# Constant rows of layer 1 from scaled sums on VectorE and products with ones, the first counting round partly in line, and five waits moved

## The chip, the cores and the metric

The kernel runs on one core of one Trainium2 chip. A core has TensorE (matrix products, 128 x 128), VectorE, ScalarE and GpSimd (elementwise work on 128 partitions), SyncE (whose queue starts the DMA transfers here), an SBUF and a PSUM of eight banks of 128 x 512 float32. Each engine has its own instruction stream and meets the others only at semaphores. The metric is the time of the whole launch in device microseconds, the median of three runs.

## The reference

A node matrix x (1024 x 512) passes four residual layers over one graph of 32768 edges, each `x = layernorm(x + layer(x))`:

```
layer 0: adj = 1 where an edge runs either way, + I; scaled by 1/sqrt(degree); adj @ (x @ W0) + b0
layer 1: three graph convolutions in a row without a nonlinearity:
         h = A (x W1) + b1;  h = A (h W2) + b2;  h = A (h W3) + b3
         A = D^-1/2 (counts of edges + I) D^-1/2
layer 2: attention: softmax over the edges of (x Wq + bq)(x Wk + bk)^T / sqrt(512), times (x Wv + bv)
layer 3: relu(A (x W1) + b1), then A (h W2) + b2
```

## The kernel before

**Layer 1 folded.** Because layer 1 has no nonlinearity, its three weights are multiplied into one matrix (units `w12`, `wf`), and the biases become constant rows: `fold1 = b2 W3` and `fold2 = (b1 W2) W3`, each needed on all 128 partitions. Before the change unit `bT` turns the two biases into columns, unit `bw` forms b1 W2 as a column (16 products of one output column each, L653), unit `g` multiplies the two columns with W3 (four products with two weight columns and 512 moving ones, L648), and the 2 x 512 result goes by DMA to DRAM and back, spread over the partitions (L465 to L468).

**The counting round.** The dense count matrix is built from the sorted edges in 64 groups of 512 edges. For each group VectorE and ScalarE make one-hot matrices (`hot_key`, `lo_near` on VectorE; `apart`, `lo_far` on ScalarE), TensorE multiplies them (L697), and VectorE adds the two results at places that are read from a table `base_at` into registers, once for four groups (L1370, L1362). VectorE makes one-hots three groups ahead. Nearly always one round of 64 groups is enough; `rounds` says how many there are.

**Units between the groups.** The dense products that don't need the graph are cut into units of four pieces. A planner deals the pieces out behind the groups of the round (`pieces`): every piece has a weight (`weight_of`), each group brings a credit of `SHARE`, and what is left stands behind the round (`BEHIND`) or between the eight transpositions of the link matrix (`REST`, L742). ScalarE copies every unit's bank out.

**Behind the round.** VectorE turns the counts into `link` (L1422), TensorE transposes it (`turn_links`), VectorE makes `sym`, and layer 0 begins (L770). Layers 1 and 3 stand twice in the program, for small and for large degrees (`big`), each as one `If` and `Else`.

**The softmax of layer 2.** For each of eight tiles VectorE finds the peak and the reciprocal, ScalarE makes exponents and quotients, and TensorE transposes the result (`turn_probs`, L983) between products of the scores (`scores`, seven products M1 to M7 of a fast matrix scheme) and of the mixing (`mix`). All three orders are written out by hand.

## Time and profile before

| | |
|---|---|
| runs, median (lowest to highest) | 546.02 us (545.72 to 546.28) |
| the profiled execution's own time | 545.62 us |
| its span in the profile | 543.8 us |
| TensorE busy | 529.8 us, 97% of the span |
| VectorE busy | 398.3 us, 73% |
| ScalarE busy | 171.7 us, 32% |
| GpSimd busy | 143.1 us, 26% |

The span runs from the first to the last instruction of the execution that the profiler recorded; its own time is 1.8 us longer, for what lies around it. Times in the rows below are microseconds from the span's start. L12 is line 12 of the kernel before. A group of instructions is given with its operation, what it writes and reads, and its count; what stands in brackets behind a row is how long its engine sat idle before it and what ended that ("issue": nothing that the profile shows).

### The profile page before, as it was taken

The numbers are of one execution on the slowest core, as the hardware profiler recorded it, in microseconds if no ns is written. First come the engines' busy times: TensorE is split into PE (matmuls) and PEld (weight loads), VectorE is DVE, ScalarE is ACT, GpSimd is POOL, SyncE is SP. The second block draws the span as 40 slices with busy tenths as digits, with TensorE's granted clock in tenths as the row PEclk, the third lists the DMA queues.
The fourth block names the chain that finished last, engine by engine and source line by source line (L and its number), as shares of the span: only waits on it lengthen the run. The fifth ranks groups of instructions, "written<-read, shape, count | busy, mean of one in ns | idle before, by whom it ended". The sixth has DMA issues, their size and how long they took to land.

```text
span 543.8 us, 7062 instructions
## 1 busy us (share of the span) xinstructions
PE 529.8 (97%) x2317; PEld 373.1 (69%) x2317; DVE 398.3 (73%) x873; ACT 171.7 (32%) x361; POOL 143.1 (26%) x135
## 2 busy tenths in 40 slices
PE   8999999999999999999999999899989999999995
PEld 6555565357788888888674764467678888888643
DVE  6888888789878989355576977897887916690165
ACT  5999896472021022220220000542343100120200
POOL 3000000085228504022224800653400390000021
PEclk9999999999999999999999999999999999999999
DMA  8724000100102012000000000000020300000012
GB/s 290 272 79 153 3 1 0 42 1 0 41 9 107 2 19 79 0 1 0 2 1 0 2 0 0 1 0 1 2 77 0 136 0 1 1 1 0 1 58 99
DMA packets 12763, 20.19 MB, mean 37 GB/s; under 512 B 3243, under 2 KB 3507, under 8 KB 12726
## 3 DMA queue, kind: packets, MB, share of 16 engines
q1 hardware_dynamic: 12726, 19.69, 10.7%
q8 instruction: 24, 0.39, 0.3%
q14 instruction: 13, 0.11, 0.1%
HBM read 17.57 MB, written 2.11 MB: 36 GB/s over the span
## 4 chain that ended last, share of the span: by engine, by line
PE 83%; DVE 8%; ACT 4%; issue 3%; POOL 1%; DVEq 0%; POOLq 0%; ACTq 0%
PE bank L951 13%; PE bank L770 13%; PE bank L955 12%; PE bank L788 11%; PE bank L1011 9%; PE bank L844 4%; PE bank L658 3%; PE bank L697 3%; PE bank L643 3%; PE bank L662 3%; PE bank L666 3%; PE bank L983 1%; DVE wk_rows L1519 1%; PE bank L674 1%; ACT apart L1101 1%
## 5 line engine op out<-in xcount | busy, mean ns | idle before, releaser
L549 POOL TENSOR_TENSOR rstd<-veps,mhalf 128x1 f32<-128x1 f32 x32 | 22.2, 695 | 177.5 <-DVE veps L1450 174.7
L1370 DVE TENSOR_TENSOR count<-bank,count 128x160 f32 x128 | 41.3, 323 | 13.9 <-PE bank L697 7.2
L788 PE MATMUL bank<-adj,y_hi 128*128 128x512 f32 x128 | 51.1, 399 | 0.0
L788 PE MATMUL bank<-adj,y_lo 128*128 128x512 f32 x128 | 50.4, 394 | 0.0
L1457 DVE SCALAR_TENSOR_TENSOR xs<-bank,dinv,xs 128x512 f32<-128x512 f32 x23 | 16.9, 746 | 43.9 <-PE bank L844 30.5
L1101 ACT ACTIVATE apart<-col_lo,edge_key 128x128 bf16<-128x128 int16 x128 | 44.0, 395 | 0.7 <-PE bank L686 0.7
L586 POOL TENSOR_SCALAR mask<-count 128x1024 bf16<-128x1024 uint16 x8 | 23.5, 2931 | 52.3 <-DVE peak L1669 43.5
L1354 DVE TENSOR_TENSOR hot_key<-col_key,key 128x320 bf16<-128x320 int16 x128 | 35.4, 316 | 0.2 <-issue 0.2
L697 PEld LDWEIGHTS bank<-hot_key,lo_near 128*128 128x128 bf16 x128 | 12.0, 100 | 31.8 <-issue 23.4
L658 PE MATMUL bank<-w_sb,x0t 128*128 128x512 f32 x64 | 33.1, 601 | 0.6 <-ACT x0t L1082 0.3
L1108 ACT ACTIVATE lo_far<-apart,ones 128x256 bf16<-128x256 bf16 x64 | 31.9, 500 | 0.0
L534 POOL TENSOR_SCALAR degs<-degs 128x1 f32<-128x1 f32 x8 | 3.5, 441 | 101.1 <-DVE sym L1427 100.7
L788 PEld LDWEIGHTS bank<-adj,y_hi 128*128 128x128 f32 x128 | 24.0, 188 | 6.1 <-DVE wide L1535 0.2
L788 PEld LDWEIGHTS bank<-adj,y_lo 128*128 128x128 f32 x128 | 24.0, 188 | 5.6
L844 PE MATMUL bank<-v_sb,gt 128*128 128x512 f32 (+1 forms) x72 | 27.6, 545 | 0.0
L1535 DVE TENSOR_TENSOR score<-bank,score 128x512 f32<-128x512 f32 x28 | 18.8, 687 | 9.9 <-PE bank L955 9.7
L770 PE MATMUL bank<-ya_hi,sym 128*128 128x512 f32 x64 | 25.4, 397 | 0.0
L770 PE MATMUL bank<-ya_hi,adj 128*128 128x512 f32 x64 | 25.2, 394 | 0.0
L788 PE MATMUL bank<-adj,yb_lo 128*128 128x512 f32 x64 | 25.2, 394 | 0.0
L788 PE MATMUL bank<-adj,yb_hi 128*128 128x512 f32 x64 | 25.2, 394 | 0.0
L770 PE MATMUL bank<-ya_lo,adj 128*128 128x512 f32 x64 | 25.1, 391 | 0.0
L770 PE MATMUL bank<-yb_lo,adj 128*128 128x512 f32 x64 | 25.0, 391 | 0.0
(288 smaller groups left out, 1241.2 us busy)
## 6 DMA issues: line engine op xcount, KB each, us to landing
w_sb<-in_L_gnn_W_dram SPq DMA_DIRECT2D x3, 1024.0 KB, 5.6
xs<-in_x_dram SPq DMA_DIRECT2D x2, 1024.0 KB, 7.1
v_sb<-in_L_gnn_W_dram SPq DMA_DIRECT2D x2, 1024.0 KB, 6.0
out_dram<-xs SPq DMA_DIRECT2D x7, 256.0 KB, 2.0
w_sb<-in_L_gnn_weight_dram SPq DMA_DIRECT2D x4, 256.0 KB, 6.1
wq_sb<-in_L_gnn_Wq_dram SPq DMA_DIRECT2D x1, 1024.0 KB, 10.6
wk_sb<-in_L_gnn_Wk_dram SPq DMA_DIRECT2D x1, 1024.0 KB, 12.8
wq_rows<-in_L_gnn_Wq_dram SPq DMA_DIRECT2D x1, 1024.0 KB, 7.8
```

Of the source, the lines that this page charges most:

```text
L658: mm = pe.matmul(to, x0t[:, k, rows], w0_sb[:, k, :], start=first, stop=last)
L697: return pe.matmul(bank[:, slot, span], lo, hot_key[:, slot, c // PAIR, :, c % PAIR], start=c % PAIR == 0, stop=c % PAIR == PAIR - 1)
L770: mm = pe.matmul(to, m[:, k, j * P:(j + 1) * P], y[part][:, k, :], start=n == 0 and part == 0 and m is mat, stop=n == NB - 1 and part == 1 ...
L788: mm = pe.matmul(to, y[part][:, k, f * P:(f + 1) * P], m[:, k, half], start=n == 0 and part == 0 and m is mat, stop=n == NB - 1 and part = ...
L844: mm = pe.matmul(bank[:, 0 if cols is high_cols else HALF * (s % 2) + b, cols], g(k, j), w[:, k, cols], start=k == 0, stop=k == FB - 1)
L951: mm = pe.matmul(to[:, i * D // 2:(i + 1) * D // 2], b[:, k, rows], a[:, k, :], start=k == 0, stop=k == 1)
L955: mm = pe.matmul(to, a[:, k, n * P:(n + 1) * P], b[:, k, :], start=k == 0, stop=k == 1)
L1011: mm = pe.matmul(mix_bank(m), left[:, k, :], right[:, k, :], start=k == 0, stop=k == HALF - 1)
L1101: ins = nc.scalar.activation(apart[:, n, c - BY_DVE, :], col_lo[:], ACT.Abs, scale=-1.0, bias=edge_key[:, 0, bass.ds(g + c * G, 1)])
L1108: nc.scalar.activation(lo_far[:, slot], apart[:, n], ACT.Relu, scale=-1.0, bias=ones[:, 0:1]).then_inc(act_hot_set, 1)
L1354: V.tensor_tensor(hot_key[:, slot, n], col_key[:], key16[:, bass.ds(g, 1), n * PAIR:(n + 1) * PAIR].to_broadcast([P, KEYS, PAIR]), ALU.is_ ...
L1370: return V.tensor_tensor(count[:, :, bass.ds(at_dst, WIN)], bank[:, slot, n * KEYS:(n + 1) * KEYS].rearrange("p (h d) -> p h d", h=NB), co ...
```

## The change

- `fold1` and `fold2` come without the DMA. VectorE forms sums over the four 128-row blocks of a weight, each block scaled per partition by the bias (`scaled_sum`, `rows_of_biases`): four instructions for b1 W2, four for b2 W3, four for (b1 W2) W3. Units `ra` and `rb` then multiply each sum with a matrix of ones, which adds over the partitions and puts the result on all of them; unit `tc` does the same with one column of ones for b1 W2, which is needed as a column. Units `bT`, `bw` and `g` are gone. The biases are loaded as columns, element by element.
- VectorE's sums stand behind twelve groups of the round (`ROWS_AT`). For that the last 32 of the 64 groups stand in line (16 before), and the first round stands ahead of the loop over rounds; the further rounds are under an `If`, which VectorE passes at the end of the first.
- The number of rounds is found behind the first one-hots, not ahead of them.
- Unit `wf` 0 comes into the round; behind it is unit `rb`. The first three link transpositions wait for their own banks' units only, not for the last.
- The large-degree copies are cut into four smaller `If`/`Else` pairs, with the products `part` standing once between them.
- Softmax: TensorE has the product M1 of tile pair 2 ahead of the first `turn_probs`; ScalarE has `exponents(1)` ahead of `first_part("s", 2)` and `quotients(6)` ahead of `first_mix(2)`; VectorE has `reciprocal(6)` ahead of `add_m57(1)`.

```diff
+ROWS_AT = (33, 35, 37, 39, 41, 43, 45, 47, 53, 55, 57, 59)
...
-        UNITS = x_t[:4] + sum((along[n] for n in range(5)), []) + [("bT", 0, 0)] + along[5]
+        UNITS = x_t[:4] + sum((along[n] for n in range(6)), [])
         UNITS += each("m") + along[6] + along[7]
-        UNITS += [("bw", 0, 0)] + each("w12") + [("g", 0, 0)] + each("wf")
+        UNITS += each("w12")[:1] + [("tc", 0, 0)] + each("w12")[1:] + [("ra", 0, 0)] + each("wf")[:1] + [("rb", 0, 0)] + each("wf")[1:]
...
-                sp.dma_start(brow[n * FB:(n + 1) * FB, :], b.rearrange("(c p) -> c p", p=P)).then_inc(cols_in, 16)
+                sp.dma_start(bcol[:, n, :], b.rearrange("(c p) -> p c", p=P),
+                             allow_slow_non_contiguous=True).then_inc(cols_in, 16)
...
-            sp.wait_ge(unit_out, upto["g"])
-            sp.dma_start(fold_rows[:, :], grow).then_inc(fold_kept, 16)
-            sp.wait_ge(fold_kept, 16)
-            for n, t in enumerate((fold1, fold2)):
-                sp.dma_start(t[:], fold_rows[n, :].partition_broadcast(P)).then_inc(fold_in, 16)
...
+                    pe.wait_ge(row_sums, {"tc": 1, "ra": 2, "rb": 3}[kind])
+                    if kind == "tc":
+                        for c in range(FB):
+                            mm = pe.matmul(to[:, c:c + 1], w2_row[:, c * P:(c + 1) * P], ones[:, 0:1], start=True, stop=True)
+                    else:
+                        mm = pe.matmul(to, ones[:], (fold1 if kind == "ra" else fold2)[:], start=True, stop=True)
...
-                if h == 0:
-                    pe.wait_ge(unit_out, UA + 1)
+                if h < 3:
+                    pe.wait_ge(unit_out, UA - 2 + h)
...
-            def layer1(mats):
...
+            whole_or_apart(lambda more: cols_steps(2, adj, yb, NB, more), rest_l1)
+            for n in range(FOLDED):
+                part(*PARTS[n])
+            whole_or_apart(layer1_rows, rest_l1)
...
+            scores(2, ("M1",))
             turn_probs(0)
-            scores(2, ("M1", "M2", "M6"))
+            scores(2, ("M2", "M6"))
...
             copy_probs(0)
+            exponents(1)
             first_part("s", 2)
-            exponents(1)
...
+            quotients(6)
             first_mix(2)
-            quotients(6)
...
+            def scaled_sum(to, w, by, k):
+
+                if k == 0:
+                    ins = V.tensor_scalar(to, w[:, 0, :], by[:, 0:1], None, ALU.mult)
+                else:
+                    dve.wait_ge(dve_set, chain[0])
+                    ins = V.scalar_tensor_tensor(out=to, in0=w[:, k, :], scalar=by[:, k:k + 1], in1=to,
+                                                 op0=ALU.mult, op1=ALU.add)
...
+            dve.wait_ge(rounds_set, 1)
+            open_round(0)
+            count_rounds()
+            dve.wait_ge(const_set, 3)
+            with dve.Fori(0, G // BODY - 2) as q:
...
+            for n in range(G - 2 * BODY, G):
+                if n % HALF == 0:
+                    places = places_at(n)
+                one_group(n, places[n % HALF], n, n % SLOTS, n + AHEAD if n + AHEAD < G else None)
+                rows_of_biases(n)
+            dve.wait_ge(rounds_set, 2)
+            rounds = dve.value_load(flags[0:1, 0:1], min_val=1, max_val=ROUNDS)
+            with dve.If(rounds > 1):
+                with dve.Fori(1, rounds) as r:
...
             m4("s", 3)
+            reciprocal(6)
             add_m57(1)
-            reciprocal(6)
```

On TensorE, the end of the round before (L697 are the groups' one-hot products, L662 unit `w12`, L648 unit `g`):

```order
L697 MATMUL bank<-hot_key,lo_far 128x160 x2
L662 MATMUL bank<-w1t,w_sb 128x512
L697 MATMUL bank<-hot_key,lo_near 128x160 x2
L697 MATMUL bank<-hot_key,lo_far 128x160 x2
L648 MATMUL bank<-w_sb,gcol 2x512
L697 MATMUL bank<-hot_key,lo_near 128x160 x2
L697 MATMUL bank<-hot_key,lo_far 128x160 x2
L648 MATMUL bank<-w_sb,gcol 2x512
```

and the same place now (L685 the one-hot products, L650 `w12`, L639 `ra`, L654 `wf`):

```order
L685 MATMUL bank<-hot_key,lo_far 128x160 x2
L650 MATMUL bank<-w1t,w_sb 128x512
L685 MATMUL bank<-hot_key,lo_near 128x160 x2
L685 MATMUL bank<-hot_key,lo_far 128x160 x2
L639 MATMUL bank<-fold_131,ones 128x512
L654 MATMUL bank<-w_sb,w12t 128x512
L685 MATMUL bank<-hot_key,lo_near 128x160 x2
L685 MATMUL bank<-hot_key,lo_far 128x160 x2
L654 MATMUL bank<-w_sb,w12t 128x512
```

The four products of `g` are gone from the last groups; one product of `ra` and the first unit of `wf`, which stood behind the round, are there instead.

On VectorE, the end of the round before (count additions of the last group, then `counted` and the link matrix):

```order
L1370 ISA
L1370 TENSOR_TENSOR count<-bank,count 128x8x20
L1388 REGISTER_ALU
L1388 COMPARE_AND_BRANCH
L1410 ISA
L1411 MEMSET rr 128x8
L1422 TENSOR_SCALAR link<-count 128x1024 x8
```

and now, where the rows left out are the 322 of the further rounds, which the branch passes over:

```order
L1358 TENSOR_TENSOR count<-bank,count 128x8x20
L1431 TENSOR_LOAD flags
L1431 ISA x2
L1432 COMPARE_AND_BRANCH
L1433 UNCONDITIONAL_BRANCH
...
L1432 UNCONDITIONAL_BRANCH
L1444 ISA
L1445 MEMSET rr 128x8
L1456 TENSOR_SCALAR link<-count 128x1024 x8
```

A load of the number of rounds and a taken branch over a long stretch of instructions have come between the last addition and the link matrix.

On TensorE, the first transpositions of probabilities now (L974, L983 before), where one product pair L943 (M1) stood behind the first of them before:

```order
L943 MATMUL bank<-xt_sums,tt 128x512 x4
L943 MATMUL bank<-xt,tt 128x512 x2
L974 MATMUL bank<-ident,score 128x128 x8
L943 MATMUL bank<-xt,tt 128x512 x2
L943 MATMUL bank<-xt_sums,tt_sums 128x512 x2
L974 MATMUL bank<-ident,score 128x128 x8
```

M1 has moved ahead of the first transposition; the second stands behind the same products as before.

## Rows read from the trace of the kernel before

**Rows 1.** the page's first part: busy time, share of the span, instructions
```profile
PE 529.8 (97%) x2317; PEld 373.1 (69%) x2317; DVE 398.3 (73%) x873; ACT 171.7 (32%) x361; POOL 143.1 (26%) x135
```

**Rows 2.** the waits of TensorE, whole span: total us, times, longest
```profile
PE bank L983 <- ACT score L1224: 3.2, 3, 1.5
```

**Rows 3.** groups of TensorE's instructions, busy us and mean ns
```profile
L648 PE MATMUL bank<-w_sb,gcol 128*2 128x512 f32 x8 | 3.9, 592 | 0.0
L653 PE MATMUL bank<-bcol,w_sb 128*128 128x1 f32 x32 | 3.8, 240 | 0.0
```

**Rows 4.** the chain: start us, us on it, what
```profile
79.17 0.79 PE bank L653 x8
```

**Rows 5.** timeline of TensorE, end of the round: start us, us, what
```profile
103.39 3.63 PE L666 MATMUL bank<-w_sb,w12t 128*128 128x512 f32 x8
107.70 0.62 PE L742 MATMUL bank<-identb,link 128*128 128x128 bf16 x8 [0.68 <-ACT wfold L1095]
```

**Rows 6.** timeline of VectorE, the round: first count of a group
```profile
60.45 0.33 DVE L1370 TENSOR_TENSOR count<-bank,count 128x160 f32 x1 [1.16 <-issue]
...
65.81 0.32 DVE L1370 TENSOR_TENSOR count<-bank,count 128x160 f32 x1 [0.61 <-issue]
...
71.16 0.33 DVE L1370 TENSOR_TENSOR count<-bank,count 128x160 f32 x1 [0.61 <-issue]
...
82.10 0.33 DVE L1370 TENSOR_TENSOR count<-bank,count 128x160 f32 x1 [0.70 <-issue]
...
88.01 0.32 DVE L1370 TENSOR_TENSOR count<-bank,count 128x160 f32 x1 [0.25 <-issue]
```

**Rows 7.** timeline of VectorE, end of the round
```profile
103.77 0.79 DVE L1370 TENSOR_TENSOR count<-bank,count 128x160 f32 x2 [1.42 <-PE bank L697]
104.61 0.41 DVE L1422 TENSOR_SCALAR link<-count 128x1024 bf16<-128x1024 uint16 x1
...
104.94 2.43 DVE L1422 TENSOR_SCALAR link<-count 128x1024 bf16<-128x1024 uint16 x7
```

**Rows 8.** groups of VectorE's instructions, busy us and mean ns
```profile
L1867 DVE TENSOR_SCALAR hidden<-hidden,dinv 128x512 f32<-128x512 f32 x8 | 3.9, 482 | 0.4 <-ACT y_hi L1292 0.4
```

**Rows 9.** timeline of VectorE, behind the round
```profile
140.19 0.75 DVE L1457 SCALAR_TENSOR_TENSOR xs<-bank,dinv,xs 128x512 f32<-128x512 f32 x1 [0.78 <-DVE flags L1488]
...
151.72 2.74 DVE L1417 SCALAR_TENSOR_TENSOR yb_lo<-xs,dinv,yb_hi 128x512 fp32r<-128x512 f32 x4 [1.90 <-ACT yb_hi L1188]
```

**Rows 10.** timeline of TensorE, where layer 1's branch lands
```profile
266.24 1.25 PE L863 MATMUL bank<-ident,xs 128*128 128x128 f32 x10
268.60 0.87 PE L863 MATMUL bank<-ident,xs 128*128 128x128 f32 x6 [1.11 <-issue]
```

**Rows 11.** timeline of TensorE in the softmax, its three waits and a product behind them
```profile
344.66 1.09 PE L983 MATMUL bank<-ident,score 128*128 128x128 f32 x8 [1.20 <-ACT score L1224]
...
351.35 1.09 PE L983 MATMUL bank<-ident,score 128*128 128x128 f32 x8 [0.45 <-ACT score L1224]
...
403.97 1.09 PE L983 MATMUL bank<-ident,score 128*128 128x128 f32 x8 [1.51 <-ACT score L1224]
...
414.41 1.89 PE L1011 MATMUL bank<-vv,prob_high 128*128 128x256 f32 x8
```

**Rows 12.** timeline of ScalarE, the softmax
```profile
347.51 0.59 ACT L1200 COPY score<-bank 128x512 f32<-128x512 f32 x1 [0.70 <-PE bank L955]
347.99 1.15 ACT L1216 ACTIVATE score<-score,peak 128x1024 f32<-128x1024 f32 x1
...
350.15 1.15 ACT L1224 ACTIVATE score<-score,esum 128x1024 f32<-128x1024 f32 x1 [0.92 <-DVE esum L1675]
...
402.77 1.15 ACT L1224 ACTIVATE score<-score,esum 128x1024 f32<-128x1024 f32 x1
```

**Rows 13.** timeline of VectorE, the softmax
```profile
398.99 0.15 DVE L1675 RECIPROCAL esum<-esum 128x1 f32<-128x1 f32 x1
...
413.62 0.41 DVE L1748 TENSOR_TENSOR half_sum<-bank,half_sum 128x256 f32<-128x256 f32 x1
```

More of the change, by code:

```diff
@@ L310, in gnn_kernel @@
         for n, (kind, _, _) in enumerate(UNITS):
-            if kind == "bw":
-                ORDER += [(m, k) for k in range(4) for m in (n, n + 1)]
-            elif kind == "xw":
+            if kind == "xw":
                 turns = [(m, k) for m in (n - 2, n - 1) for k in range(4)]
@@ L325, in weight_of @@
             kind = UNITS[ORDER[m][0]][0]
-            return TURNED if kind[-1] == "T" else D // 2 if kind == "bw" else FB * P * 2
+            if kind in ("tc", "ra", "rb"):
+                return (TURNED if kind == "tc" else FB * P * 2) if ORDER[m][1] == 3 else 0
+            return TURNED if kind[-1] == "T" else FB * P * 2
         def ended(m):
@@ L621, in piece @@
                 to = unit_bank(n)
-                if k == 0 and n >= 4:
+                if k == (3 if kind in ("tc", "ra", "rb") else 0) and n >= 4:
                     pe.wait_ge(unit_out, n - 3 if n < NU - 1 else UA + 1)
@@ L643, in piece @@
                     mm = pe.matmul(to, wqt[:, k, rows], wkt[:, k, :], start=first, stop=last)
-                elif kind == "g":
-                    pe.wait_ge(w_in["3"], 16)
-                    pe.wait_ge(unit_out, upto["bw"])
-                    mm = pe.matmul(to[0:2, :], gcol[:, k, :], w3_sb[:, k, :], start=first, stop=last)
-                elif kind == "bw":
-                    pe.wait_ge(w_in["2"], 16)
-                    for c in range(FB):
-                        mm = pe.matmul(to[:, k:k + 1], w2_sb[:, c, cols], bcol[:, 0, c:c + 1],
-                                       start=c == 0, stop=c == FB - 1)
                 elif kind == "xw":
@@ L956, in part, with whole_or_apart, layer1_rows @@
                 mm.then_inc(part_done, 1)
-            def layer1(mats):
-                more = mats[1] if len(mats) > 1 else None
-                cols_steps(2, adj, yb, NB, more)
-                for n in range(FOLDED):
-                    part(*PARTS[n])
+            def whole_or_apart(steps, rest):
+                with pe.If(big < 1):
+                    steps(None)
+                with pe.Else():
+                    steps(rest)
+            def layer1_rows(more):
                 for half in range(2):
@@ L1055, in _, with layer3_first @@
             mixes(3, MIXES)
-            def layer3(mats):
-                more = mats[1] if len(mats) > 1 else None
+            def layer3_first(more):
+                if more is not None:
+                    pe.wait_ge(rest_set, 2)
                 cols_steps(10, adj, y3, 4 * NB, more, TILES)
-                for n in range(IN_LAYER2, len(PARTS)):
-                    part(*PARTS[n])
-                cols_steps(12, adj, y3, 5 * NB, more, PAIRS)
-                pe.wait_ge(w_in["v2"], 16)
-                for half in range(2):
-                    weight_step(14 + half, half, by_cols(gt3), v2_sb, 12 + half)
-            with pe.If(big < 1):
-                layer3([adj])
-            with pe.Else():
-                pe.wait_ge(rest_set, 2)
-                layer3([adj, rest_l3])
+            whole_or_apart(layer3_first, rest_l3)
+            for n in range(IN_LAYER2, len(PARTS)):
+                part(*PARTS[n])
+            whole_or_apart(lambda more: cols_steps(12, adj, y3, 5 * NB, more, PAIRS), rest_l3)
+            pe.wait_ge(w_in["v2"], 16)
+            for half in range(2):
+                weight_step(14 + half, half, by_cols(gt3), v2_sb, 12 + half)
         @block.scalar
@@ L1160, in _ @@
                 copy_unit(n)
[L1161 removed]
+            act.wait_ge(unit_done, upto["w12"])
             for k in range(NB):
@@ new lines, in _ @@
+            dve.wait_ge(rounds_set, 2)
+            rounds = dve.value_load(flags[0:1, 0:1], min_val=1, max_val=ROUNDS)
+            with dve.If(rounds > 1):
+                with dve.Fori(1, rounds) as r:
+                    open_round(r)
+                    with dve.Fori(0, G // BODY - 1) as q:
+                        for n in range(BODY):
+                            if n % HALF == 0:
+                                places = places_at(q * BODY + n)
+                            one_group(q * BODY + n, places[n % HALF], r * G + q * BODY + n, n % SLOTS, q * BODY + (n + AHEAD))
+                    for n in range(G - BODY, G):
+                        if n % HALF == 0:
+                            places = places_at(n)
+                        one_group(n, places[n % HALF], r * G + n, n % SLOTS, n + AHEAD if n + AHEAD < G else None)
```

91 lines of the change are left out of this document (44 added, 47 removed).

## The prediction

> **What bounds the kernel now.** I read the page's busy shares first: TensorE is busy for 97% of the span [rows 1], so by the page a microsecond of TensorE's work removed is a microsecond won. Then its waits, whole span: the largest is 3.2 us in three pieces, for ScalarE's quotients in the softmax [rows 2]. Both say TensorE. But the share is an average, and the work that goes lies in the counting round, so that stretch is read by itself, on VectorE's timeline. From group 36 to group 40 VectorE takes 5.35 us and sits idle for only 0.61, at the load of the next four places [rows 6]; the same 0.61 stands ahead of each four groups in the loop, with nothing but "issue" behind it. So VectorE runs the round flat out up to group 48 (82.10), and TensorE is merely dealt as much work as fits. Only the last 16 groups, in line, are set by TensorE; VectorE waits for its last products by 1.42 us [rows 7]. The round has two bounds that nearly coincide, and the change takes from one and gives to the other.
>
> Behind the round the chain is: last addition (103.77 + 0.79), eight link instructions to 107.37 [rows 7], first transposition at 107.70, after 0.68 us of waiting for ScalarE's copy of `wf` 0 [rows 5]. Unit `wf` 0, 3.63 us from 103.39, fills TensorE's time meanwhile.
>
> **TensorE's part.** Removed: `g` 3.9 us [rows 3]; `bw` four times the chain's 0.79 [rows 4], 3.2 (its busy 3.8 overlaps). Added: `tc`, eight records like the eight of [rows 4], 0.8; `ra` and `rb`, two records of 512 columns each, at `g`'s 3.9/8 = 0.5 a record, 1.0 each. Net: 7.1 - 2.8 = 4.3 us less work. `wf` 0 (3.6) moves into the round, so inside it there is 7.1 - 0.8 - 1.0 - 3.6 = 1.7 less, behind it 2.6 less. The 2.6 brings nothing: TensorE has to wait there for the link matrix, and will show idle time in place of `wf`. From the 1.7 alone the round would end at 102.9 instead of 104.56.
>
> **VectorE's part.** Added: three scalings of 128x512 at 0.48 [rows 8] and nine multiply-adds at 2.74/4 = 0.685 [rows 9], 7.6 us. Nearest rows, both from SBUF and in float32. What it gains: group 32 came after 1.16 idle at the loop's return; it will be a loop's exit, as group 48 was, with 0.70, so group 32 starts at 60.45 - 0.46 = 60.0. A group without load takes (5.35 - 0.61)/4 = 1.185. In line, the load cost 0.25 (group 52 [rows 6]); six of the sums stand right ahead of a load and should cover that, since the load goes on in the sequencer while the engine works off what it has. Groups 32 to 47: 16 x 1.185 + 2 x 0.48 + 6 x 0.685 = 24.0, to 84.0 (82.10 before). From 48: thirteen groups with one-hots 15.4, three without at about half of 0.79 + 0.1, 1.5, four sums 2.5, one load 0.25: 19.7, to 103.7. Before: 104.56. Bounds: 102.9 if TensorE's side is the later one after all, 105.2 if no load is covered (6 x 0.25). I take 103.7: **0.9 earlier**.
>
> **The branch behind the round.** New between the last addition and the link matrix: a load of a flag and a taken branch over 322 rows. A flag's load kept VectorE 0.78 us [rows 9]; it is issued while the last addition runs, which hides about 0.4 of it, so 0.4 is left. The branch has no like on VectorE. Lower bound: the loop's return cost 1.16 - 0.61 = 0.55 [rows 6], a branch to instructions run shortly before. Upper: TensorE's far branch at the end of layer 1, over the large-degree copy, landed on ten transpositions, and then stood 1.11 us idle for "issue": 268.60 - 266.24 = 2.36 us until the rest came [rows 10], and work queued ahead of it may have hidden more, so 3.3 is my outer bound. VectorE's branch is that kind (far, forward, never run before) and has half a microsecond of work queued. I take 2.1. Sum: **2.5 later** (0.9 to 3.7). Everything waits for it: link matrix, transpositions, `sym`, layer 0.
>
> The Trainium skill ("Runtime: NRT & Kernel Launch", section "Instruction fetch mechanics") says that prefetch is sequential and that a taken branch out of the two-page window waits for a fetch by DMA. By that rule the far branch can't be cheap and all four of the new far branches pay; the row of layer 1's branch agrees for TensorE, for VectorE no row here shows it. By the rule the sum would lie at my upper values.
>
> **The three waits on banks.** The 0.68 behind the round [rows 5] goes, since `turn_links` no longer waits for the last unit: **0.7 earlier**. Together the start of layer 0 moves by -0.9 + 2.5 - 0.7 = +0.9.
>
> **Softmax.** M1 (1.7 us) fills the 1.20 ahead of the first transposition [rows 11]. But the second waits for `quotients(1)` (350.15), and that doesn't come earlier: `exponents(1)` ran at 347.99 and can gain at most the 0.48 of the copy ahead of it (347.51) [rows 12]; now that copy (0.59) comes behind it, and VectorE's addition of M2 waits for the copy and stands ahead of the reciprocal. 347.6 + 1.24 + 0.6 + 0.7 + 0.4 gives about 350.3, 0.15 later. So the wait at 351.35 grows from 0.45 to about 1.8: **+0.1**. The third, 1.51 at 403.97: the reciprocal at 398.99 [rows 13] stood behind additions that waited for M7, the quotient (402.77) behind a copy that waited for M4. Both are freed; the wait goes. Next late is VectorE's half sum (413.62 + 0.41), on which the product at 414.41 depends; VectorE comes earlier by about 1.0 only, so some 0.3 returns: **-1.2**. Softmax: -1.1.
>
> **The cut copies.** Three more far branches on TensorE. They land on products whose records last about twice as long as those ten transpositions' 1.25/10, so ten of them cover the 2.36; TensorE's own queue is full when it branches. I take +0.1, outer bounds 0 and 3 x 1.11 = 3.3. The DMA through DRAM was hidden (VectorE asks for it some 70 us later), and the biases' element-wise load is needed only at group 33: nothing.
>
> **Sum.** 0.9 - 1.1 + 0.1 = -0.1 against the profiled execution's own 545.62 (span 543.8 plus 1.8), whose time is 0.4 below the median of the runs: 546.02 - 0.1 = 545.9.
>
> **Rivals.**
> - *The far branch on VectorE is cheap* (0.5, as the loop's return), because its target is fetched by the time the load is done. Then 1.6 more is won: 544.3; with TensorE's side of the round at 102.9 as well, 543.5. For: the loop's returns are cheap. Against: [rows 10].
> - *Every far branch stalls*: also the three new ones on TensorE at 1.11 each, 545.9 + 3.2 = 549.1. This ends slower, and decides from two of the three on. For: the one such branch that the trace shows does stall, with TensorE as full as elsewhere. Against: slower records behind it.
> - *VectorE's sums cost more than in the rows*: no load covered (+1.5), TensorE starved between groups 36 and 48 and unable to catch up, 547.4.
> - *The softmax gives more, and layer 1's old branch lands well*: the 1.11 of [rows 10] depends on where it lands, and code in front of it has changed. 544.6.
> - *The page's reading*: TensorE is the bound everywhere, 4.3 us of work and the softmax's 1.1 go, 540.6. Against: [rows 6], VectorE's 0.61 a load.
>
> **How the numbers follow.** Three runs of this kernel spread by 0.56 us; I call 0.2% (1.1 us) the least that counts as a change. Chances: forecast 0.39 (545 to 547); cheap branch 0.22; all branches 0.15; dear sums 0.12; better softmax and landing 0.09; page's reading 0.03. Faster: 0.22 + 0.09 + 0.03 = 0.34, less 0.01 that falls within, 0.33; slower 0.15 + 0.12 = 0.27 with 0.01 less, 0.26; the same 0.41. The range 543.4 to 548.2 leaves out the page's reading and the fullest stall. The likeliest case's own range is 544.9 to 547.1.
>
> **What the changed profile would show.** TensorE: no unit `bw` or `g`, an idle stretch of 3 to 5 us ahead of the first link transposition, put down to VectorE's link. VectorE: between groups 33 and 60 no idle for places, groups 36 to 48 at about 6.0 us a four; a gap of 2 to 3 us of "issue" between the last addition and the first link instruction. If that gap is under 1 us, I am wrong towards faster. The second softmax wait grows to about 1.8 and the first and third are gone. "Issue" ahead of TensorE's first products behind each `Else` would be the second rival.

## The result and the profile after

| | before | after |
|---|---|---|
| runs, median (lowest to highest) | 545.94 us (545.48 to 546.30), 8 runs | 548.70 us (548.03 to 550.63), 8 runs |
| profiled execution, its span | 545.62, 543.8 us | 548.54, 546.7 us |

The changed kernel is slower by 0.54% (ratio 1.0054, 95% interval 1.0045 to 1.0064): 2.8 us, where 0.1 less was forecast, and above the range's upper end of 548.2. The page of after, its first part, shows less work on TensorE than [rows 1] by only 0.1 us, in a span that is 2.9 longer:

```profile
PE 529.7 (97%) x2288; PEld 372.2 (68%) x2288; DVE 404.6 (74%) x885; ACT 172.6 (32%) x360; POOL 142.6 (26%) x135
```

TensorE issues 29 products fewer and is busy for almost as long, so something made others slower. The waits of TensorE of after, as in [rows 2]:

```profile
PE bank L730 <- DVE link L1456: 4.1, 1, 4.1
PE bank L974 <- ACT score L1211: 2.3, 2, 1.9
```

One wait of 4.1 us, for the link matrix. The timeline of VectorE of after (start, us, what), first the round's counts of groups 36, 40, 48 and 52 as in [rows 6], then the round's end as in [rows 7]:

```profile
65.53 0.32 DVE L1358 TENSOR_TENSOR count<-bank,count 128x160 f32 x1
...
71.48 0.32 DVE L1358 TENSOR_TENSOR count<-bank,count 128x160 f32 x1
...
83.36 0.32 DVE L1358 TENSOR_TENSOR count<-bank,count 128x160 f32 x1
...
88.30 0.32 DVE L1358 TENSOR_TENSOR count<-bank,count 128x160 f32 x1 [0.23 <-issue]
...
103.09 0.79 DVE L1358 TENSOR_TENSOR count<-bank,count 128x160 f32 x2 [0.20 <-DVE count L1358]
107.28 0.07 DVE L1445 MEMSET rr<- 128x8 f32 x1 [3.40 <-issue]
107.29 2.78 DVE L1456 TENSOR_SCALAR link<-count 128x1024 bf16<-128x1024 uint16 x8
```

The round went as worked out: 5.95 us for four groups with two sums, the loads covered, the last addition done at 103.88. Then VectorE stands for 3.40 us with nothing but "issue". The timeline of TensorE of after, the same place as in [rows 5] and on to layer 0 (L758):

```profile
102.65 1.10 PE L639 MATMUL bank<-fold,ones 128*128 128x512 f32 x2 [0.54 <-ACT wfold L1082]
107.86 2.54 PE L730 MATMUL bank<-identb,link 128*128 128x128 bf16 x8 [4.11 <-DVE link L1456]
110.32 2.04 PE L654 MATMUL bank<-w_sb,w12t 128*128 128x512 f32 x2
112.16 1.06 PE L730 MATMUL bank<-identb,link 128*128 128x128 bf16 x8
113.01 2.02 PE L654 MATMUL bank<-w_sb,w12t 128*128 128x512 f32 x2
...
116.50 0.61 PE L730 MATMUL bank<-identb,link 128*128 128x128 bf16 x8
116.95 1.08 PE L654 MATMUL bank<-w_sb,w12t 128*128 128x512 f32 x2
...
126.34 0.79 PE L758 MATMUL bank<-ya_hi,sym 128*128 128x512 f32 x1
```

Two products of `wf` take 2.04 us at 110.32 and 1.08 at 116.95: the same instruction on the same operands, at half speed. The windows of after (from:to, length, busy us of PE, PEld, DVE, ACT, POOL, then the granted clock) name it:

```profile
102.00:104.00 2.00, 1.21 (x4) 0.30 (x2) 1.31 (x4) 0.67 (x2) 0.00 (x0) 1.00 0.01 4
104.00:106.00 2.00, 0.00 (x0) 0.00 (x0) 0.00 (x0) 0.37 (x1) 0.00 (x0) 0.81 0.02 4
106.00:108.00 2.00, 0.14 (x1) 0.10 (x1) 0.72 (x4) 0.56 (x1) 0.00 (x0) 0.50 0.01 4
...
112.00:114.00 2.00, 2.00 (x11) 1.32 (x10) 0.74 (x1) 1.21 (x2) 1.10 (x3) 0.50 0.03 8
114.00:116.00 2.00, 2.00 (x11) 1.13 (x10) 0.70 (x3) 0.95 (x2) 1.22 (x3) 0.63 0.00 0
116.00:118.00 2.00, 2.00 (x15) 1.03 (x14) 2.00 (x4) 1.15 (x2) 0.81 (x2) 1.00 0.00 0
```

In the idle stretch that `wf` 0 had filled before, TensorE's clock fell from full (2.4 GHz) to 0.50 (1.2 GHz). It stood there for about 10 us by these windows and came back between 7 and 8 us after work had begun again. Layer 0 starts at 126.34 in place of 121.63, 4.7 us later. The rest of the program is quicker than before: 420.36 us from layer 0's start to the span's end against 422.17. Layer 1's branch lands without a stall (TensorE's timeline of after; [rows 10] had two pieces with 1.11 between them):

```profile
270.90 1.91 PE L851 MATMUL bank<-ident,xs 128*128 128x128 f32 x16
```

and in the softmax the first and third waits of [rows 11] are gone, the second has grown, and one has come up that was not there:

```profile
348.54 1.04 PE L974 MATMUL bank<-ident,score 128*128 128x128 f32 x8
...
354.91 1.09 PE L974 MATMUL bank<-ident,score 128*128 128x128 f32 x8 [1.90 <-ACT score L1211]
...
371.06 1.09 PE L974 MATMUL bank<-ident,score 128*128 128x128 f32 x8 [0.41 <-ACT score L1211]
...
406.48 1.04 PE L974 MATMUL bank<-ident,score 128*128 128x128 f32 x8
```

### The profile page after: what moved, and what is told of

Same layout as the page of the kernel before. It is cut to its first block, busy times and chain, and to the rows that moved or that the text cites. A ratio compares the mean times of both kernels' runs of the same rounds, so it can differ in the third digit from the quotient of the medians.

```text
span 546.7 us, 6950 instructions
## 1 busy us (share of the span) xinstructions
PE 529.7 (97%) x2288; PEld 372.2 (68%) x2288; DVE 404.6 (74%) x885; ACT 172.6 (32%) x360; POOL 142.6 (26%) x135
## 4 chain that ended last, share of the span: by engine, by line
PE 76%; DVE 13%; issue 5%; ACT 3%; DVEq 1%; POOL 1%; POOLq 0%; ACTq 0%
PE bank L939 13%; PE bank L758 13%; PE bank L943 11%; PE bank L776 11%; PE bank L1002 8%; PE bank L832 4%; PE bank L654 3%; PE bank L650 3%; DVE count L1358 2%; PE bank L646 2%; PE bank L685 2%; DVE hot_key L1342 1%; DVE wk_rows L1553 1%; PE bank L662 1%; ACT apart L1088 1%
## 5 line engine op out<-in xcount | busy, mean ns | idle before, releaser
L685 PEld LDWEIGHTS bank<-hot_key,lo_near 128*128 128x128 bf16 x128 | 12.1, 98 | 34.7 <-issue 24.7
L646 PE MATMUL bank<-w_sb,x0t 128*128 128x512 f32 x64 | 33.0, 600 | 0.6 <-ACT x0t L1072 0.3
L758 PE MATMUL bank<-ya_hi,sym 128*128 128x512 f32 x64 | 25.4, 397 | 0.0
L758 PE MATMUL bank<-ya_hi,adj 128*128 128x512 f32 x64 | 25.2, 394 | 0.0
L758 PE MATMUL bank<-ya_lo,adj 128*128 128x512 f32 x64 | 25.1, 391 | 0.0
L758 PE MATMUL bank<-yb_hi,adj 128*128 128x512 f32 x64 | 25.0, 391 | 0.0
```

The costliest lines, as they stand in the source:

```text
L646: mm = pe.matmul(to, x0t[:, k, rows], w0_sb[:, k, :], start=first, stop=last)
L758: mm = pe.matmul(to, m[:, k, j * P:(j + 1) * P], y[part][:, k, :], start=n == 0 and part == 0 and m is mat, stop=n == NB - 1 and part == 1 ...
```

## The experiments

Executions differ at their beginning: the first product with `x0t` (L646 of after) starts between 11.7 and 16.2 us. So beside the median each run is read from its trace in two stretches, which leave that out: from that first product to the start of layer 0 ("to layer 0"), and from there to the end of the span ("behind"). The kernel before ran beside each set of them, with medians of 545.99 to 546.10. The medians are over all executions of a kernel; each stretch is read from the one execution that was profiled, and so is the gap, VectorE's idle time ahead of the memset behind the branch.

| kernel | median us | runs | gap on VectorE | to layer 0 | behind |
|---|---|---|---|---|---|
| before | 545.94 | 8 | none | 109.38 | 422.17 |
| changed | 548.70 | 8 | 3.40 | 114.25 | 420.36 |
| filler products | 549.02 | 10 | 3.32 | 111.50 | 421.46 |
| `wf` 0 behind again | 548.90 | 10 | 3.73 | 113.08 | 420.42 |
| no load, no branch | 544.93 | 10 | 0 | 109.91 | 420.42 |
| load earlier | 547.83 | 10 | 2.65 | 113.22 | 420.42 |
| near branch | 545.89 | 10 | 0.63 | 110.58 | 420.36 |
| first softmax pair back | 547.73 | 10 | 3.40 | 114.15 | 419.72 |
| old `If`s | 549.47 | 4 | 3.45 | 112.98 | 420.38 |
| before, bank waits alone | 545.87 | 10 | none | 109.03 | 422.35 |
| link ahead of the branch | 546.82 | 10 | 0.78 | 111.82 | 420.40 |
| the same, filler | 545.07 | 10 | 0.78 | 109.56 | 421.40 |
| the same, filler, pair back | 543.82 | 12 | 0.79 | 109.57 | 419.69 |
| three sums of twelve | 546.52 | 10 | 3.30 | 111.51 | 420.45 |
| short further rounds | 546.24 | 10 | 1.08 | 110.75 | 420.38 |
| short, filler, pair back | 543.35 | 12 | 1.07 | 109.32 | 419.70 |
| longer start | 544.92 | 12 | 1.04 | 109.75 | 420.61 |

### What the idle stretch costs

Filler products:

```diff
             for m in BEHIND:
                 piece(m)
+            pe.wait_ge(unit_out, UA - 2)
+            for k in range(FB):
+                pe.matmul(bank[:, HALF, :], w12t[:, k, 0:P], w3_sb[:, k, :], start=True, stop=True)
```

> The changed kernel, with four products of 128 x 512 (eight records, some 3.6 us, into a bank that is free) in TensorE's idle stretch of 4.1 us ahead of the first link transposition; nothing else moved. Theory A (the idle stretch lets TensorE's clock fall to 0.50 and that costs): the clock stays at 1.00 from 104 to 116 us, the first transposition still waits for VectorE's link matrix and starts at about 107.9, but layer 0 starts some 2.5 us earlier (near 123.8 in place of 126.3), and the time falls from 548.7 to about 546.2. Theory B (layer 0 is late because the link matrix is late, and VectorE and ScalarE pace the transpositions anyway): layer 0 starts near 126.3 whatever the clock is, the time stays within 0.5 us of 548.7.

TensorE's timeline of this kernel, the idle stretch:

```profile
105.71 3.60 PE L738 MATMUL bank<-w_sb,w12t 128*128 128x512 f32 x8
109.98 2.48 PE L730 MATMUL bank<-identb,link 128*128 128x128 bf16 x8 [0.68 <-DVE link L1459]
112.44 1.10 PE L654 MATMUL bank<-w_sb,w12t 128*128 128x512 f32 x2
```

The gap on VectorE is as long, the link matrix still paces the first transposition (2.48 us), but `wf` runs at full speed, and the way to layer 0 is 2.75 us shorter in the two profiled executions, by products whose results nobody reads: theory A. The median, 549.02 where 546.2 was expected, shows none of it. In the profiled execution (549.18) two things took the gain back: its beginning was 2.4 us longer, and at 355.43 the clock fell once more, behind the softmax wait of 1.91. TensorE's timeline and window there:

```profile
355.43 3.25 PE L1005 MATMUL bank<-vv,prob_low 128*128 128x256 f32 x8
```
```profile
356.00:358.00 2.00, 2.00 (x6) 1.60 (x5) 1.93 (x5) 0.64 (x1) 0.77 (x1) 0.50 0.00 0
```

In the changed kernel these eight products take 1.89. The runs of this kernel reach from 545.64 to 555.98; without the two above 555 the median is 548.4. The three fastest (545.64 to 546.20) are where theory A had them, and 2 us below the changed kernel's fastest, 548.03. The four slowest have a mean granted clock of 0.990 to 0.993 over the span, the three fastest 0.998 and 0.999; where theirs fell is not shown. So the gain is shown up to layer 0, and for the whole kernel in a part of the executions only. The clearer pair in the medians comes below: the kernel with the link matrix ahead of the branch, with and without the same filler (546.82 and 545.07 us; nine of ten at 545.47 to 547.30 against eight of ten at 543.97 to 545.64; to layer 0 111.82 and 109.56).

What the clock costs is best read from the memset behind the gap, which releases the transpositions, to the start of layer 0. With filler products this takes 16.53 us, here and in the kernel with short rounds, filler and the pair back, and the clock stays at 1.00. Where TensorE idled for 3.4 to 4.2 us it takes 19.06 in the changed kernel and with the first softmax pair back, 18.52 with the load earlier, 18.22 with three sums and 17.85 with the old `If`s, in all five with the clock at 0.50 for a while. The windows of the last of these have it there for about 7 us and not 10. Nearly the same idle stretch thus cost between 1.3 and 2.5 us, and the changed kernel's profiled execution is at the upper end.

Useful work in its place (the planner stops ahead of `wf`, and `rb` is dealt only once `g` is past 61):

```diff
-... + [("ra", 0, 0)] + each("wf")[:1] + [("rb", 0, 0)] + each("wf")[1:]
+... + [("ra", 0, 0), ("rb", 0, 0)] + each("wf")
...
-            while credit > 0 and m < len(ORDER) - 4:
+            while credit > 0 and UNITS[ORDER[m][0]][0] != "wf" and (UNITS[ORDER[m][0]][0] != "rb" or g > 61):
```

> The changed kernel with unit wf 0 behind the round again and unit rb inside it: useful work in the idle stretch in place of idle. Theory A (clock): the same gain as with filler products, 2.5 us, to about 546.2; nothing more, since wf 0 was done in the round behind VectorE's pace. Theory B (late link alone): no gain, 548.7. If the round ends later than 103.9 because TensorE has wf 0's work at another place, neither: then TensorE's work inside the round counted.

To layer 0 1.2 us are won, not 2.75. TensorE ran short inside the round instead (idle 0.49, 0.69, 0.43 and 1.13 us between 101.8 and 106.4), had `wf` 0 done at 110.1 and stood for another 1.79; the clock fell to 0.50 for 114 to 116. Here the moved work only moved the idle time; this run tells little beyond that.

### The gap on VectorE

No load, no branch (further rounds left out on VectorE), and the load ahead of group 60:

```diff
-            dve.wait_ge(rounds_set, 2)
-            rounds = dve.value_load(flags[0:1, 0:1], min_val=1, max_val=ROUNDS)
-            with dve.If(rounds > 1):
...
+            dve.wait_ge(win_added, G + 2)
```

> The changed kernel without the further rounds on VectorE: no flag load, no branch (on this graph they are not run, so the outputs are those of the full kernel; for a graph that needs more rounds they would be wrong). Theory A: the gap of 3.4 us between last addition and link matrix goes, TensorE's idle stretch shrinks to about 0.7 us and its clock doesn't fall: 3.3 (less the 0.3 that it meets otherwise) plus 2.5, the time falls by 5 to 5.8 us to about 543.2. Theory B (no clock cost): it falls by the 2.7 to 3.3 us alone, to about 545.7. Theory C (the gap is not the branch but something else behind the last addition, such as the wait or the memset): the gap stays.

> The changed kernel with the load of the number of rounds moved ahead of the last four groups; the If and its branch stay where they are. If the gap of 3.4 us is nearly all the branch's instruction fetch, it shrinks by at most 0.4 and the time stays at 548.3 to 548.7. If the load is half of it, the gap falls to 2 us or less, TensorE's clock may stay up, and the time falls by 1.5 to 4 us. My forecast: gap 3.0, time 548.4.

Without both the gap is 0 (theory C falls) and the way to layer 0 4.3 us shorter. That is 3.4 for the gap and only 0.9 of the clock's 2.5: the clock fell here too (0.50 between 108 and 110), with only 0.83 us of idle time ahead of the transposition but 2.48 us in which TensorE does eight small transpositions at VectorE's pace. With the load moved, the gap is 2.65, where I had expected 3.0 and at most 0.4 less than before: by this difference the load is 0.75 of the 3.40, the rest the branch.

Near branch (the `If` holds one memset; further rounds left out):

```diff
             with dve.If(rounds > 1):
-                with dve.Fori(1, rounds) as r:
...
+                V.memset(shift[:], 0.0)
```

> The changed kernel with the body of VectorE's If cut down to one memset: the flag load and a taken branch stay, but it jumps over one instruction and not over 322 rows (further rounds left out, as in the run without load and branch). Theory A (the distance matters: the target's code has to be fetched): the gap behind the last addition falls from 3.4 us to about 1.3 (the load's 0.75 plus a near jump of 0.55), the link matrix comes 2.1 us earlier. Theory B (any taken branch costs the same, the pipeline of the sequencer): the gap stays at 3.4. Theory A's time: about 546, between the kernel without branch (543.4 at its best) and the changed one.

VectorE's timeline of this kernel behind the last addition (102.81 + 0.79):

```profile
104.23 0.07 DVE L1435 MEMSET rr<- 128x8 f32 x1 [0.63 <-DVE count L1358]
```

The same load and a taken branch over one instruction cost 0.63 together, half of what theory A had, and over 322 rows 3.40: theory A. The 0.63 is less than the 0.75 that the load was given above, so that split is a difference between two kernels and no fixed price of the load. This kernel also loses the arithmetic on `rounds` in the wait behind the branch. The next edit keeps it and changes only what is passed over: the further rounds are written shorter (for every graph the same result):

```diff
-                    with dve.Fori(0, G // BODY - 1) as q:
-                        for n in range(BODY):
+                    with dve.Fori(0, G // HALF - 1) as q:
+                        for n in range(HALF):
...
-                    for n in range(G - BODY, G):
+                    for n in range(G - HALF, G):
```

> The changed kernel with VectorE's further rounds written shorter: their loop holds 4 groups in place of 16, and 4 groups stand behind it in place of 16, so the branch passes over 91 rows and not 322; it computes the same for every graph. Known so far: over 322 rows the gap is 3.40 us, over one instruction 0.63. Theory A (the target is already fetched when it is near enough): the gap is 0.6 to 0.9, the time that of the near jump, 545.9. Theory B (each stretch passed over costs): the gap is about 0.63 plus 2.77 times 91/322, 1.4. Theory C (a jump out of what is fetched costs the same whatever its length, and 91 rows are out of it): 3.4 as before, 548.7.

```profile
105.08 0.07 DVE L1445 MEMSET rr<- 128x8 f32 x1 [1.08 <-issue]
```

VectorE's timeline has 1.08 over 91 rows. Theory C (3.4 as before) is out. The number is neither of the others': 0.45 over the near jump where B had 0.78 and A at most 0.27. The three points (1, 91 and 322 rows) lie on no line, and the DMA view says why a line is the wrong picture. The changed kernel's queue of instructions, between the last addition and the memset (103.8 to 107.4):

```profile
q14 instruction: 2, 0.02, 1.5%
```

The first of the two transfers starts at 103.9 and has its like in the other kernels too, also in the one without a branch (103.4). The second starts at 105.2, 2.1 us ahead of the memset. I compared eight profiled kernels that jump over 322 rows (changed, filler products, `wf` 0 behind again, load earlier, first pair back, old `If`s, link ahead of the branch, three sums): in each of them such an 8 KB transfer starts 1.9 to 2.4 us ahead of the memset. In the two kernels with 91 rows and in the one with a single instruction none starts between the one at the end of the additions and the memset. So the long jump has an instruction transfer in its gap and the short ones have not. 2.3 of the 3.4 us go with it, and only 0.45 lies between the two short jumps. That VectorE waits for this transfer is inferred; the view doesn't say which engine asked for it. From what distance on a jump needs one lies between 91 and 322 rows and may depend on where the code stands; no run here settles that.

Link matrix ahead of the branch, remade inside the `If` where there are further rounds:

```diff
+            dve.wait_ge(win_added, G + 2)
+            made = make_link(link_made)
             dve.wait_ge(rounds_set, 2)
             rounds = dve.value_load(flags[0:1, 0:1], min_val=1, max_val=ROUNDS)
             with dve.If(rounds > 1):
...
+                dve.wait_ge(make_link(link_again), NB)
+            dve.wait_ge(made, NB)
+            V.memset(rr[:, 0:HALF], 0.0).then_inc(counted, 1)
+            V.memset(rr[:, HALF:NB], 0.0).then_inc(link_set, NB)
```

> The changed kernel with the eight link instructions (2.8 us of VectorE's work) ahead of the flag's load and branch; where there are further rounds they are followed by a second making of the link matrix, so it computes the same for every graph. The branch's 3.4 us should lie beside those 2.8 us: link matrix done at about 106.7, released with the branch at 107.3 in place of 110.1, the first transposition done at 107.8 in place of 110.3. TensorE still idles 4 us ahead of it, so its clock should fall as in the changed kernel. Theory A: 2.5 us earlier, 546.2. Theory B (the sequencer can't run ahead, or the fetch starts only when the engine is done): load and branch follow the link instructions, release at 110, no gain.

VectorE's timeline of this kernel:

```profile
104.14 2.78 DVE L1433 TENSOR_SCALAR link<-count 128x1024 bf16<-128x1024 uint16 x8
107.70 0.06 DVE L1455 MEMSET rr<- 128x4 f32 x1 [0.78 <-DVE link L1433]
```

Load and branch run beside the link instructions, and 0.78 of them is left. To layer 0 2.4 us are won: theory A. The kernel before had shown such a branch already. Its VectorE passes over the sixteen instructions of `make_rest` ahead of the memset of L1499, behind a `normalise` that ends at 148.84:

```profile
148.79 0.06 DVE L1499 MEMSET degmax<- 128x1 f32 x1
```

There, with work queued ahead of a short jump, it lost nothing.

### The softmax, the `If`s, the bank waits, the sums

The first softmax pair put back, the old single `If` and `Else` of layers 1 and 3, and the kernel before with only its bank waits changed:

```diff
-            scores(2, ("M1",))
             turn_probs(0)
-            scores(2, ("M2", "M6"))
+            scores(2, ("M1", "M2", "M6"))
...
-            exponents(1)
             first_part("s", 2)
+            exponents(1)
```

> The changed kernel with the first softmax pair put back: M1 of tile pair 2 behind the first transposition of probabilities, ScalarE's exponents(1) behind its copy. By my sum the pair brings 1.20 at the first wait and loses 1.45 at the second: waits of 1.2 and 0.45 in place of 0 and 1.9, so the product of the first mix starts 0.2 us earlier and the time stays within 0.3 us. Theory B: the 1.9 us wait at the second also lets TensorE's clock fall in some executions (it did in the run with filler products, at 355.4: eight products took 3.25 us in place of 1.89), so with the pair put back no execution shows a low clock between 350 and 362, and the slowest of its times are nearer to its median. Theory C (the pair is worth its 1.2): 1 us slower.

TensorE's waits are 1.19 and 0.45 again, and the one at 371 is gone. The stretch behind layer 0's start is 0.64 us shorter than in the changed kernel. Putting it back was to bring 0.2 and brings 0.64: the pair cost that much.

```diff
-            whole_or_apart(lambda more: cols_steps(2, adj, yb, NB, more), rest_l1)
...
+            with pe.If(big < 1):
+                layer1([adj])
+            with pe.Else():
+                layer1([adj, rest_l1])
```

> The changed kernel with layers 1 and 3 again as one If and Else each. Theory A (where layer 1's branch lands decides, and cutting it in four moved the landing): the stall of 1.1 us for issue in the transpositions of layer 1 is there again, and the time is 1.1 to 1.3 us longer, 549.9. Theory B (code in front of it has moved the landing, the cut did nothing): no stall, 548.7.

No stall, 420.38 behind against 420.36: theory B by the trace. The median of the four runs, 549.47, lies nearer to theory A's 549.9, but they reach from 548.00 to 550.90, and the profiled one is the 548.00 and has no stall; I go by the trace. By it the cut of the copies costs and brings nothing, and its new branches on TensorE are free. They are two and not three: four `If`/`Else` pairs in place of two.

```diff
-                if h == 0:
-                    pe.wait_ge(unit_out, UA + 1)
+                if h < 3:
+                    pe.wait_ge(unit_out, UA - 2 + h)
```

> The kernel before with nothing changed but the bank waits of the first three link transpositions. My term was 0.68 us earlier. Theory A: the first transposition starts 0.6 to 0.7 us earlier, at about 107.0, layer 0 too, and the time falls to about 545.4. Theory B (it frees TensorE earlier only to wait for VectorE or ScalarE at one of the next steps, or lowers the clock): layer 0 starts at 121.6 as before, no change.

The first transposition starts 0.68 us earlier against the first `x0t` product (94.77 against 95.45), layer 0 only 0.35: the eight transpositions now go at the link matrix's pace. 545.87 us, ratio 0.9999 (0.9987 to 1.0011): nothing to be measured.

Three sums of twelve:

```diff
-                scaled_sum((w2_row, fold1, fold2)[n][:], ...)
+                if k == FB - 1:
+                    scaled_sum((w2_row, fold1, fold2)[n][:], ...)
```

> The changed kernel with three of VectorE's twelve sums left (each a scaling of one block; nine multiply-adds of 0.67 net left out, so the constant rows of layer 1 are wrong). If VectorE's work sets the end of the round, the round ends up to 6 us earlier until TensorE's side takes over; my sum put TensorE's side at 102.9 against VectorE's 103.7, so the last addition should end near 102.9 to 103.1, 0.8 to 1.0 us earlier, and no more. If it ends at 98 to 99, TensorE was far from being the bound; if at 103.9, VectorE's sums cost nothing.

The last addition ends at 101.93 in place of 103.88 and now waits for TensorE's products (0.40 a group). The nine sums left out (the constant rows of layer 1 are wrong without them) are 6 us of work at 0.67 each and cost 1.95 us of time, 0.15 of which is this execution's earlier start; TensorE's side of the round stands at 101.9, a microsecond lower than I had it.

### Together

> The kernel of the run before this one and four filler products on TensorE in the idle stretch: both costs of the branch taken away, its place on the path and the clock. Layer 0 should start 16.5 less 2.4 us behind the release at 107.3, at about 121.3 (before: 121.6; changed: 126.3), so 5 us are won, 543.7. If it starts later than 122, something else (ScalarE's copies of the counts, which are released at 107.3 and not at 104.6 as before) paces the transpositions.

Layer 0 starts at 121.30, as worked out. The median is 545.07 and not 543.7: two of the ten executions are at 548.7 and 550.3, and the profiled one has a stall of 0.73 us for "issue" on TensorE (at 186.98), in a place where the changed kernel had none; behind layer 0's start it took 1.0 us more than the kernel without filler.

> The same and the first softmax pair put back, which was worth 0.8 us by its trace: 543.7 less 0.8, 542.9, so 0.5 to 0.6% faster than the kernel before and 1% faster than the changed one.

543.82 in 12 runs, eight of them between 542.95 and 543.94, four between 547.2 and 549.5; the ratio is 0.9985 (0.9956 to 1.0014), so not settled.

> The same, with the four filler products on TensorE and the first softmax pair put back. If the short branch is cheap, the first link transposition is done at about 107.3 as in the kernel with the link matrix ahead of the branch, layer 0 starts near 121.2, and the time is 543.7; ScalarE gets the counts at 104.5 in place of 107.3, which nothing waits for by the traces so far. If the branch still costs 3.4, layer 0 starts at 123.7 and the time is 545.4.

543.35 us over all twelve runs, ratio to the kernel before 0.9952 (0.9931 to 0.9974) without its two longest: 0.5% faster. TensorE's timeline of this kernel at the round's end has no idle time ahead of the link transposition:

```profile
103.11 3.60 PE L738 MATMUL bank<-w_sb,w12t 128*128 128x512 f32 x8
106.55 1.08 PE L730 MATMUL bank<-identb,link 128*128 128x128 bf16 x8
107.61 1.10 PE L654 MATMUL bank<-w_sb,w12t 128*128 128x512 f32 x2
```

Two of its twelve executions took 1110 and 1411 us, which no other kernel's did; they are not explained.

```diff
-            idle_turns(16)
+            idle_turns(19)
```

> The fastest kernel so far (link matrix ahead of the branch, filler products, first softmax pair put back), with 19 in place of 16 idle transpositions on TensorE ahead of the first key rows. Theory: the tail of its times (4 of 12 at 547 to 549.5 beside 8 at 543 to 544) comes from executions in which the edges land 0.45 us later, TensorE is idle for 0.24 us there and its clock falls until 13 us, as the profiles of two kernels show. Three more transpositions cover 0.6 us: the tail goes, at 0.2 to 0.4 us for all others. If the tail stays as thick, it has another cause or that cover is too short.

Three of twelve executions lie at 550 to 551 and the others at 543.6 to 545.7: the tail is as thick, and the first `x0t` product starts 1.0 us later (12.84 against 11.84), where I had 0.2 to 0.4. Nor is a tail peculiar to these kernels: beside the first set the kernel before had four of 31 executions at 547.8 to 550.4. The theory of the beginning has only this behind it, TensorE's timeline of the changed kernel and of the one with filler products:

```profile
6.50 0.88 PE L662 MATMUL bank<-ident 128*128 128x128 f32 x6
```
```profile
5.93 1.22 PE L674 MATMUL bank<-ident,key_rows 64*128 64x64 f32 x8 [0.24 <-ACT key_rows L1105]
7.08 1.54 PE L662 MATMUL bank<-ident 128*128 128x128 f32 x6
```

In the second the edges landed 0.45 us later, TensorE was idle for 0.24, and the six transpositions behind it took nearly twice as long. That this makes the whole tail is not shown.

## Why the prediction was wrong

The ledger of the two profiled executions, in us. "Forecast" is the sum that is on record.

| step | forecast | measured | from |
|---|---|---|---|
| round's end | -0.9 | -0.7 | 103.88 against 104.56 |
| load and far branch | +2.5 | +3.4 | gap; by the load moved, 2.65 the branch, 0.75 the load |
| bank waits | -0.7 | -0.5 | the product behind the first transposition starts 2.16 later (110.32, 108.16), the link matrix 2.68 |
| TensorE's idle stretch | 0 | +2.5 | the rest to layer 0's +4.7; release to layer 0 19.06 against 16.53 with filler |
| landing of layer 1's branch | 0 | -1.2 | a stall of 1.11 that is gone |
| softmax | -1.1 | -0.6 | 420.36 against 422.17, less the 1.2 |
| cut copies | +0.1 | 0 | old `If`s |
| sum | -0.1 | +2.9 | spans 546.7 and 543.8 |

**The step that failed** is a sentence of TensorE's part: "The 2.6 brings nothing: TensorE has to wait there for the link matrix, and will show idle time in place of `wf`." I saw the idle stretch coming (3 to 5 us, measured 4.1) and put it down at nothing. It cost 2.5 us in the profiled execution (1.3 to 2.5 over the kernels with such a stretch), because the clock falls in it and the work behind it runs at half speed for over 7 us, on the path. No rival had it either. The rival *every far branch stalls* has a time near the measured one, 549.1, and that is chance: none of its stalls came up on TensorE in the changed kernel. `wf` 0 behind the round was no work to be tidied away; it was the cover of a wait. With this term the same sum gives 548.4, close to the measured 548.7; that it comes so close is luck in part, since the branch, the bank waits, the round and the softmax were 1.8 us too favourable together and a stall that nobody had aimed at gave 1.2 back.

**The far branch** was 2.65 where I took 2.1, and the load 0.75 where I took 0.4, by the difference of the two gaps; so read, the half microsecond of the last addition hid nothing of the load. The forecast said that the branch has no like on VectorE. The one over `make_rest` is one, though short and with work ahead of it. The total, 3.4, lies inside its bounds (0.9 to 3.7), near the upper one. That such a branch is dear because it is far is shown by the shorter ones: 1.08 over 91 rows and 0.63 over one, each with its load. The Trainium skill ("Runtime: NRT & Kernel Launch", section "Instruction fetch mechanics") lets a taken branch wait for a DMA fetch when its target is outside the window of two pages that it describes. For VectorE the runs agree with that in kind: 3.40 us with an instruction transfer in the gap, 1.08 and 0.63 without. For TensorE the two new branches cost nothing (I had counted three), so the rival *every far branch stalls* is out.

**Layer 1's old branch** was half of a rival (0.09): its 1.11 us of [rows 10] was to depend on where it lands. It went, by 1.2, and with the old `If`s too; the code ahead of it had been changed by other edits, and which of them moved it is not shown. This gain belongs to no edit on purpose.

**The softmax** was right at both ends of the pairs and wrong by a wait that I had not looked for. The second wait grew to 1.90 (forecast 1.8) and the third went. But with the second transposition late, the fourth in the row, at 371.06, waits 0.41 as well, and the first pair costs 0.64 in all (forecast 0.1). A slip in the sum hid a part: 347.6, 1.24, 0.6, 0.7 and 0.4 make 350.54 and not 350.3, which gives the pair 0.4. The 0.3 forecast to return behind the third wait is there, as 0.25: the product at 417.24 starts that much behind its turn.

**The round** was right: VectorE-bound, the sums behind loads cover them, 103.88 against 103.7. Only TensorE's side was 1 us further off than I had it.

## What to carry to other kernels

Before work is taken out of a stretch in which TensorE waits, ask what its clock does there: here idle stretches of about 4 us cost another 1.3 to 2.5 behind them, and four products that nobody reads gave that back on the way to layer 0. In the medians one pair of kernels shows 1.75 us of it and the other none, so look at all executions and not at the fastest. A rare branch over a long body can be dear when it stands alone on the path, 3.40 us here over 322 rows; write the body as a short loop, or put work that can be done either way ahead of the branch. And a gain of half a microsecond in one place has to be followed to the next two waits of the same kind, not only to the next one.

## What the hardware showed that I had not expected

- The clock also fell without a long idle stretch: at 0.83 us idle and 2.48 us of eight small transpositions, each released by VectorE, it went to 0.50 a little later (kernel without branch, 108 to 110 us). Behind the softmax wait of 1.9 us it fell in one profiled execution and not in the others of the same order.
- A taken branch on VectorE and the load ahead of it run beside work that is already queued: of 3.4 us 0.78 was left behind 2.78 us of link instructions.
- Stalls of TensorE for "issue" come and go with code elsewhere: 1.11 in layer 1 before, none after, 0.73 at another place in the kernel with the link matrix ahead of the branch and filler products, none in the same kernel without the filler.
- The price of a taken branch on VectorE came in two sizes, with and without an 8 KB instruction transfer in its gap: 3.40 us over 322 rows, 1.08 over 91 and 0.63 over one, each with the load of its flag.
